# Causal masks of the latent attention: from two TensorE matmuls to VectorE and GpSimd

## The reference

```python
T, D = 2048, 256; H, LAT, RD = 16, 64, 64; HD = D // H        # 16 heads, 16 + 64 columns of a key
q  = heads(x @ Wqd @ Wqu);  qr = rope(heads(x @ Wqd @ Wqr))
k  = heads(x @ Wkvd @ Wku); v  = heads(x @ Wkvd @ Wvu); kr = rope(x @ Wkr)     # kr shared by the heads
scores = (q @ k.T + qr @ kr.T) / sqrt(HD + RD)
scores = where(key <= query, scores, -inf)
x = x + (softmax(scores) @ v) @ Wo
```

## Time and profile before

| | before |
|---|---|
| median of three runs | 3063.18 us (3056.26 to 3066.55) |
| span of the profiled execution, first to last instruction | 2911.1 us |
| TensorE busy | 2553.8 us (88%), 14687 matmuls |
| VectorE busy | 1795.2 us (62%) |
| ScalarE busy | 1474.6 us (51%) |
| GpSimd busy | 1132.5 us (39%) |
| unit 4 to unit 7 (c = 0, 1, 2, 3), first S to the next unit's first S | 36.0, 49.1, 62.9, 65.7 us |
| last unit, to its last A | 51.0 us |

### The profile page before, as it was taken

One profiled execution on the slowest core, in us unless ns is written; L12 is line 12 of the kernel. 1 busy time (PEld: TensorE's weight loads), 2 busy tenths in 40 slices (PEclk: granted clock), 3 DMA queues, 4 the chain that ended last, 5 costly groups with the idle time before them and its releaser, 6 DMA issues. The chain is left out here.

```text
span 2911.1 us, 42096 instructions
## 1 busy us (share of the span) xinstructions
PE 2553.8 (88%) x14687; PEld 1960.8 (67%) x14687; DVE 1795.2 (62%) x3458; ACT 1474.6 (51%) x2894; POOL 1132.5 (39%) x991
## 2 busy tenths in 40 slices
PE   4967999999999997696989989889868998898798
PEld 4855555555555554585877777677768887776687
DVE  7556774874865862755554897889835444445443
ACT  3435547547457455343225886868644434334232
POOL 2642211211212211362332664636346566657232
PEclk9988999999999997798999999999989999999899
DMA  4241000000000001323010000000032233323200
GB/s 158 84 141 44 16 8 23 17 9 23 18 12 15 15 2 60 96 88 119 30 37 8 1 1 8 1 8 1 8 110 86 82 89 94 92 84 100 89 1 30
DMA packets 70267, 138.64 MB, mean 48 GB/s; under 512 B 16816, under 2 KB 38024, under 8 KB 68912
## 3 DMA queue, kind: packets, MB, share of 16 engines
q0 software_dynamic: 26336, 73.01, 8.4%
q1 hardware_dynamic: 43728, 62.95, 6.5%
HBM read 114.71 MB, written 20.81 MB: 47 GB/s over the span
## 5 line engine op out<-in xcount | busy, mean ns | idle before, releaser
L1437 ACT ACTIVATE PT<-ps 128x512 f32<-128x512 f32 (+3 forms) x640 | 313.2, 534 | 283.8 <-PE ps L1190 147.9
L2288 POOL DMA_INDIRECT KV<-kv_scratch,sidx x384 | 368.6, 960 | 217.5 <-issue 131.6
L1303 DVE TENSOR_REDUCE xn<-ps 128x1 f32<-128x512 f32 (+3 forms) x640 | 342.7, 601 | 62.9 <-PE ps L1167 46.7
L35 PE MATMUL ps<-KIh,qih 128*128 128x512 f32 (+2 forms) x640 | 249.5, 390 | 50.3 <-DVE Isc L1872 40.7
L1932 POOL TENSOR_TENSOR part_sum<-part_sum,rlp 128x1024 f32<-128x1024 f32 (+7 forms) x120 | 210.7, 1755 | 89.3 <-ACT rlp L1758 88.3
L1872 DVE SCALAR_TENSOR_TENSOR Isc<-ps,iw,Isc 128x1024 f32<-128x1024 f32 (+7 forms) x216 | 208.5, 965 | 54.2 <-ACT ps L1782 48.8
L36 PE MATMUL ps<-KIl,qih 128*128 128x512 f32 (+2 forms) x640 | 240.4, 376 | 0.0
L37 PE MATMUL ps<-KIh,qil 128*128 128x512 f32 (+2 forms) x640 | 240.2, 375 | 0.0
L1187 PE MATMUL ps<-qB,KB 128*128 128x512 f32 (+2 forms) x640 | 233.9, 365 | 0.0
L2210 ACT ACTIVATE sP<-sP,snm 128x128 f32<-128x128 f32 (+2 forms) x256 | 110.4, 432 | 232.4 <-DVE snm L2273 229.3
L1782 ACT ACTIVATE ps<-ps,iwa 128x1024 f32<-128x1024 f32 (+7 forms) x240 | 198.1, 858 | 48.0 <-PE ps L37 47.6
(11 more groups left out here) (362 smaller groups left out, 6948.5 us busy)
## 6 DMA issues: line engine op xcount, KB each, us to landing
cs<-in_rope SPq DMA_DIRECT2D x20, 512.0 KB, 4.2
ycomb<-y_rows SPq DMA_DIRECT2D x16, 512.0 KB, 5.0
w1raw<-in_w SPq DMA_DIRECT2D x14, 512.0 KB, 6.5
KV<-kv_scratch,sidx POOLq DMA_INDIRECT x384
xn_rows<-xnr SPq DMA_DIRECT2D x8, 512.0 KB, 4.9
whr<-in_whead SPq DMA_DIRECT2D x16, 256.0 KB, 2.8
w2raw<-in_w SPq DMA_DIRECT2D x14, 256.0 KB, 7.0
wir<-in_wi SPq DMA_DIRECT2D x1, 2176.0 KB, 8.0
```

The costliest lines, as they stand in the source:

```text
L35: pe.matmul(out, lhs[0], rhs[0], start=start, stop=False)
L1303: v.tensor_reduce(mp[:, CT * h + r, k:k + 1], o[:, 0:end], AX_X, ALU.max).then_inc(a_free, 1)
L1437: s.activation(PT[:, rnd % 2, hh, lo:CH], ps[:, ST_BANKS[e % 3], lo:CH], ACT.Exp, scale=SCALE).then_inc(a_exp, 1)
L2288: g.indirect_dma_start(KV[:, BG * (k % RB) + m, :], None, a["kv_scratch"], bass.IndirectOffsetOnAxis(sidx[:, t % 2, at:at + 1], 0)).then_i ...
```

## The change

Both mask matmuls go. In an M step the last piece of each 128 queries is read by `tensor_tensor_reduce`: it adds to the scores a row of `cm_bf` and takes the maximum in one go. `cm_bf` now holds four blocks, three of zeros and the causal one, so that the last (r + 1) blocks fit the piece. In an S step nothing is masked; once the four exponentials of a diagonal block are there, GpSimd sets those above the diagonal to zero by `affine_select` (one instruction for the four heads) and counts `a_cut`, for which A waits as well. `mcol` and `mrow` move into parts of xn, to make room; two semaphores (`a_ve`, `a_kr`) become one (`a_kv`) with the counts 1, 9 and 10, in the order in which ScalarE raised them before.

```diff
-        cm_bf = sb("cm_bf", [P, 3, P], BF16, a_ctx)
+        cm_bf = sb("cm_bf", [P, CT, P], BF16, a_ctx)
...
-        mcol = sb("mcol", [P, GH * CT], F32, a_ctx)
-        mrow = sb("mrow", [GH * CT, P], F32R, a_ctx)
+        mcol = xn[:, 0, 6 * GH * CT:7 * GH * CT]
+        mrow = xn[0:GH * CT, 0, P:2 * P].bitcast(F32R)
...
+        def on_diagonal(u, j):
+            return j >= CT * (u % NCH)
+
+        def cut(u, j):
+            return CT * u + j - CT * (u % NCH) + 1
...
-                        i = pe.matmul(o[:, 0:wide], q, KA[h][:, CH * s:CH * s + wide], start=True, stop=s < c)
-                        if s == c:
-                            i = pe.matmul(o[:, r * P:(r + 1) * P], cm_bf[:, 2, :], cm_bf[:, 0, :], start=False, stop=True)
-                        i.then_inc(a_full, 1)
+                        pe.matmul(o[:, 0:wide], q, KA[h][:, CH * s:CH * s + wide], start=True, stop=True).then_inc(a_full, 1)
...
-                        if j >= CT * c:
-                            i = pe.matmul(o[:, lo:lo + P], cm_bf[:, 2, :], cm_bf[:, 1, :], start=False, stop=True)
...
                     pe.wait_ge(a_exp, GH * (ROUND[u, j] + 1))
+                    if on_diagonal(u, j):
+                        pe.wait_ge(a_cut, cut(u, j))
...
-                        end = min(CH, (CT * c + r + 1) * P - CH * k)
-                        v.tensor_reduce(mp[:, CT * h + r, k:k + 1], o[:, 0:end], AX_X, ALU.max).then_inc(a_free, 1)
+                        if k < c:
+                            v.tensor_reduce(mp[:, CT * h + r, k:k + 1], o, AX_X, ALU.max).then_inc(a_free, 1)
+                        else:
+                            end = (r + 1) * P
+                            seen = cm_bf[:].rearrange("p a t -> p (a t)")[:, CH - end:CH]
+                            v.tensor_tensor_reduce(out=o[:, 0:end], in0=o[:, 0:end], in1=seen, scale=1.0, scalar=LEAST,
+                                                   op0=ALU.add, op1=ALU.max, accum_out=mp[:, CT * h + r, k:k + 1]).then_inc(a_free, 1)
...
-            s.copy(cm_bf[:, 0:2, :], cm_raw)
-            s.copy(cm_bf[:, 2, :], ident[:])
+            s.activation(cm_bf[:, 0:CT - 1, :], ident[:].unsqueeze(1).to_broadcast([P, CT - 1, P]), ACT.Copy, scale=0.0)
+            s.copy(cm_bf[:, CT - 1, :], cm_raw[:, 0, :])
...
+                elif kind == "S" and r == 1 and on_diagonal(u, h):
+                    rnd = ROUND[u, h]
+                    own = PT[:, rnd % 2, :, st_start(u, h):st_start(u, h) + P]
+                    p.wait_ge(a_exp, GH * (rnd + 1))
+                    p.affine_select(own, own, [[0, GH], [1, P]], ALU.is_ge, 0.0, base=0, channel_multiplier=-1).then_inc(a_cut, 1)
```

More of the change, by code:

```diff
@@ L930, in build @@
         SCALE = float(1.0 / np.sqrt(np.float32(HD + RD)))
+        LEAST = -3e38
         BF16 = mybir.dt.bfloat16
@@ L975, in build @@
         KA = [XTh[:, 0, :], XTh[:, 1, :], XTl[:, 0, :], XTl[:, 1, :]]
-        (a_c, a_wph, a_wpl, a_ms, a_pq, a_pt, a_pd, a_rr, a_rh, a_kb, a_v, a_ve, a_kr) = (
-            sem(x) for x in ("a_c a_wph a_wpl a_ms a_pq a_pt a_pd a_rr a_rh a_kb a_v a_ve a_kr").split())
+        (a_c, a_wph, a_wpl, a_ms, a_pq, a_pt, a_pd, a_rr, a_rh, a_kb, a_v, a_kv) = (
+            sem(x) for x in ("a_c a_wph a_wpl a_ms a_pq a_pt a_pd a_rr a_rh a_kb a_v a_kv").split())
+        KEYS_LOW, VALUES, KEYS_HIGH = 1, 1 + TILES // 2, 2 + TILES // 2
         a_w = [sem("a_w0"), sem("a_w1")]
         (a_wh, a_wl, a_wo, a_woh, a_wol, a_full, a_free, a_tk, a_tq, a_qhi, a_qb, a_mc, a_md, a_st, a_exp,
-         a_av, a_vg, a_oe, a_rc, a_dn, a_rd, a_oh, a_ol) = (
+         a_av, a_vg, a_oe, a_rc, a_dn, a_rd, a_oh, a_ol, a_cut) = (
             sem(x) for x in ("a_wh a_wl a_wo a_woh a_wol a_full a_free a_tk a_tq a_qhi a_qb a_mc a_md a_st a_exp "
-                             "a_av a_vg a_oe a_rc a_dn a_rd a_oh a_ol").split())
+                             "a_av a_vg a_oe a_rc a_dn a_rd a_oh a_ol a_cut").split())
         a_csl = [sem("a_cs0"), sem("a_cs1")]
@@ L1124, in attn_tensor @@
                 else:
-                    pe.wait_ge(a_ve, max(t // 2 - 3, 0))
+                    pe.wait_ge(a_kv, KEYS_LOW + max(t // 2 - 3, 0))
                 for m in range(2):
@@ L1158, in attn_tensor @@
                     if u == 0:
-                        pe.wait_ge(a_kr, 1)
+                        pe.wait_ge(a_kv, KEYS_LOW)
                     elif u == 2:
-                        pe.wait_ge(a_kr, 2)
+                        pe.wait_ge(a_kv, KEYS_HIGH)
                     q = qA[:, par, h, r * P:(r + 1) * P]
@@ L1186, in attn_tensor @@
                         pe.matmul(o[:, mm_lo:CH], KA[hh][:, j * P:(j + 1) * P], qA[:, par, hh, mm_lo:CH], start=True, stop=False)
-                        i = pe.matmul(o[:, mm_lo:CH], KB[:, j * P:(j + 1) * P], qB[:, par, hh, mm_lo:CH],
-                                      start=False, stop=j < CT * c)
-                        if j >= CT * c:
-                            i = pe.matmul(o[:, lo:lo + P], cm_bf[:, 2, :], cm_bf[:, 1, :], start=False, stop=True)
-                        i.then_inc(a_st, 1)
+                        pe.matmul(o[:, mm_lo:CH], KB[:, j * P:(j + 1) * P], qB[:, par, hh, mm_lo:CH],
+                                  start=False, stop=True).then_inc(a_st, 1)
                 elif kind == "A":
@@ L1374, in attn_scalar @@
                 i = s.copy(KA[h][0:RD, 0:HALF], KB[0:RD, 0:HALF].bitcast(F32))
-            i.then_inc(a_kr, 1)
+            i.then_inc(a_kv, 1)
             for t in range(0, TILES, 2):
                 s.wait_ge(a_v, t // 2 + 1)
-                s.copy(V[:, t:t + 2, :].rearrange("p t d -> p (t d)"), ps[:, LAT_BANK + t // 2 % 4, :]).then_inc(a_ve, 1)
-            s.wait_ge(a_ve, TILES // 2)
+                s.copy(V[:, t:t + 2, :].rearrange("p t d -> p (t d)"), ps[:, LAT_BANK + t // 2 % 4, :]).then_inc(a_kv, 1)
+            s.wait_ge(a_kv, VALUES)
             def values(g, half):
```

2 lines of the change are left out of this document (1 added, 1 removed).

## The result

| | before | after |
|---|---|---|
| median of the runs, same chip, 20 each | 3064.74 us (3056.26 to 3077.66) | 3052.38 us (3043.87 to 3064.34) |
| ratio | | 0.9965, 95% interval 0.9954 to 0.9975 |
| first S of unit 0 to the last A | 838.2 us | 825.3 us |
| TensorE matmuls | 14687 | 14175, 512 fewer |

The change makes the kernel 0.35% faster, 12.4 us. The interval leaves no doubt that it moved, and it moved down, where the prediction said up: 3069.7 us, 6.5 us slower. The time lies in the stated range and almost on the number of its first rival, the fast select (3052 us).

The account below looks back on a forecast made before the run. It took VectorE to pace c = 0 units, TensorE c = 3 units, with c = 1 and c = 2 between. Unit terms, mask savings against select and accumulator costs, summed to +6.5 us on 3063.2: 3069.7 us, range 3050 to 3100.

Parts of the forecast that it names:

- first rival: GpSimd at diagonal blocks: a fast select of 0.53 us keeps the masks' time, -11 us, 3052 us; chance 0.25.
- The select: GpSimd at diagonal blocks: each AFFINE_SELECT takes 1.3 us, so A starts no sooner than 1.4 us after the exponentials.
- The accumulator: VectorE in M pieces: a second instruction writes the accumulator out, 0.08 us each, 1.3 us a unit, 20 us in all.
- How much of the masks reaches the path: c = 1 units: of 3.8 us of removed masks 45% comes through, 1.7 us a unit.
- the ring: Four PSUM banks for row-maximum pieces: they fill because VectorE takes longer per piece, so TensorE waits in bursts.
- block 13's 1.27 us: c = 3 units: smallest gap from last exponential to A, 710.32 to 711.59, against the 1.4 us needed.
- A mask's price on TensorE: Each removed mask matmul saves 0.12 us, follower's weight load included; 512 make 61 us, the most that can be won.
- The last unit gets slower: Last attention unit: four A each lack 1.2 to 1.35 us in series, less mask savings, +3.8 us.
- The first preparation: Before unit 0, paced by VectorE: 16 accumulator instructions at 0.08 us, +1.3 us.
- The time around the span: Outside the profiled execution's 2911.1 us: 152.1 us up to the median of the runs, taken as unchanged.
- The slow select: GpSimd at diagonal blocks: a select of 2.4 us, some 30 us more, 3100 us; chance 0.18.
- VectorE as the bound: VectorE in M pieces: accumulator at 187 ns, 16 us more, 3086 us; chance 0.12.

Follow-up runs that it names:

- the halves above: The changed kernel with two selects per diagonal block, one for each two heads, A waiting for both: ratio 0.9961, stage 822.8 us.
- the two halves: Against the kernel before: selects only, M masks left on TensorE, ratio 0.996; VectorE's mask add only, S masks left on TensorE, ratio 0.9975.
- the plain maximum: The changed kernel with the old reduction over unmasked M pieces, no accumulator: ratio 0.9934, stage 818.1 us; measured again 0.994, 818.5 us.

## Why the prediction was wrong

The sum said +6.5 us and the time moved by -12.4. Two terms of the sum were too large, both on the costly side, and they made the sign wrong; that A waits for the select, and that VectorE has a second instruction, was right as a mechanism.

- **The select, 1.3 us taken, 0.64 measured.** This is the step that failed first: of the rows of GpSimd I took the add of as many elements (1.29 us), because it too reads and writes. The row that came out nearest was the fill, 0.53 us. With 1.4 us to A instead of 0.80, c = 2, c = 3 and the last unit were forecast at +6.0 together and came to -4.2; the kernel with two selects returns them to +6.5, though not unit by unit. Between the two kernels the stage differs by 10.3 us (14 without after's episode), where the first rival had 17.7. The Trainium skill, GPSIMD Engine Reference, Engine selection (4.1), calls one-input operations roughly line rate; by my estimate from the clock that the page states, 0.43 us and dispatch, it was much nearer than the row that I chose. The trace agrees for this instruction (0.46 us for 512 elements by the halves above, and 0.18 on top), and not for TENSOR_SCALAR in the earlier trace rows.
- **The accumulator, 0.08 us a piece taken, about 0.01 measured.** I took the length of a small instruction as its price. Its length is even more, 0.14 us, but the next one starts beside it. c = 0 and c = 1 units were forecast at -0.8 together and came to -8.9. Of the 2.6 us that I had held against c = 1 and the 3.6 of c = 0 little can be there: taking the accumulator away changes these units by -0.8 and +0.8 us, as much as they scatter.
- **How much of the masks reaches the path.** I let 45% through in c = 1, 1.7 us a unit; measured are 1.9, half of the 3.8, with hardly anything for VectorE to take back. In c = 3 the two halves gain 2.0 and 4.2 us apart and 3.0 together (about 5 without the episode). That VectorE and the ring take back a part was right, and it doubled PE's wait for banks, as above.
- **A gap read wrongly.** For c = 3 the prediction called block 13's 1.27 us the smallest gap. Unit 7 of before has a smaller one on the diagonal: the last exponential of block 14 ends at 714.88, its A starts at 715.22, 0.34 us later. How the three blocks take back 3.4 us is not worked out there either, so that this term can't be checked. In after the gaps of blocks 12 to 14 are 1.23, 0.81 and 1.04 us there, and a c = 3 unit pays 0.6 us for the select.
- **A mask's price on TensorE, 0.12 us: right where a matmul follows at once**, at the rows of after and with doubled masks, and too large as a mean: the busy time fell by 0.07 us a mask, so the ceiling of 61 us was nearly twice too high. The Trainium skill, TensorE: Matmul & The Clock Gate, Back-to-back issue gap, gives 56 ns for a single matmul of 128 columns; the second of two masks, 0.056 us, agrees with that, and the first, with its follower, costs twice as much.
- **The last unit gets slower: right in sign**, +1.6 for +3.8. Four floors of 0.80 us in place of 0.25, 0.12, 0.23 and 0.05 are 2.6 us, less the 1.2 that its masks are worth: 1.4. Over before it stands at -1.2 without selects, +0.6 with halves, +1.6 as changed, +5.2 with two.
- **The first preparation**, +1.3 forecast and +1.8 measured, is VectorE's for less than half. The same kernel with the plain maximum took 31.1 us there once and 32.1 the second time, and the clock goes with it: the granted clock of this stretch is 0.83 in before (31.0 us) and in the first of these traces, 0.75 in the second and in after (32.9). So about 1 us stands with the clock, and 0.8 us (32.9 for 32.1, at 0.75 both) with the accumulator; 16 x 0.01 us from start to start doesn't explain it. Which wait makes it stays open.
- **The time around the span** was no 152.1 us but 1.7 us; the rest is, as far as the lengths tell, the difference between two chips. It cancelled in the sum, which was made as a difference, so it cost nothing here.
- **The rivals.** The slow select and VectorE as the bound are excluded by the 636 ns and by c = 0 units of 35.7 us. The first rival's number was met, but not with its terms: it put more on the select (17.7 us for 10.3 to 14) and kept VectorE's 9.1, of which 3 to 4 were there. What made up the difference was not measured apart; the episode's 3.8 us is a part of it. So the agreement with 3052 us is luck in part. The chance of 0.25 for a fast select was too low for the row of the fill that I had beside it, and with it the chance of 0.22 for faster.

## What to carry to other kernels

When an instruction isn't in the trace, lay the rows of its engine out by what they do per element, and let the range of prices, not the one that seems alike, decide the chances: here 0.7 us more of one instruction, at the diagonal blocks where little hides it, was the whole gain. Price an operation by the start of what follows it, a small companion instruction above all, and read the price of a short matmul from the step of its follower too, where one follows at once. Two savings on the engine that leads are not additive once its follower is near: ask after the first what it will wait for, and undo a change just where its new wait has nothing beside it, as in the last unit. Before a difference of a few us in a stage is given to a change, look for late DMAs and for the granted clock in both traces, and compare stretches that have neither.
